# GpSimd and ScalarE put the bias into PSUM in place of a bias matmul, in two large dense layers of a GNN and MoE kernel

## The reference

```
# L0_ffn: 8 experts, hidden 1024, top-2 gates
h = gelu_tanh(einsum('td,edh->teh', x, W1) + b1[None])
y = einsum('teh,eho->teo', h, W2) + b2[None];  out = einsum('te,teo->to', gates, y)
# L2_ffn: 8 experts, hidden 2048, gates from a binary tree of sigmoids
h = gelu(einsum('nd,edh->neh', x, w1) + b1[None])
y = einsum('neh,ehd->ned', h, w2) + b2[None];  out = einsum('ned,ne->nd', y, leaf_probs)
```

## Time and profile before

| what | value |
|---|---|
| three timed runs | 589.77, 591.35, 594.08 us; median 591.35 |
| span of the profiled execution, first to last instruction | 590.4 us |
| median less span | 0.95 us |
| TensorE clock granted, mean | 0.988 |
| PE, DVE, ACT, POOL busy | 557.9, 490.8, 412.2, 15.7 us |
| L0F pipeline, by the chain | about 26.7 to 134.2 us |
| L2F pipeline, by the chain | about 223.7 to 428.1 us |
| L3F pipeline, by the chain | about 468.8 us to the end |

### The profile page before, as it was taken

One profiled execution on the slowest core, in us unless ns is written; L12 is line 12 of the kernel. 1 busy time (PEld: TensorE's weight loads), 2 busy tenths in 40 slices (PEclk: granted clock), 3 DMA queues, 4 the chain that ended last, 5 costly groups with the idle time before them and its releaser, 6 DMA issues.

```text
span 590.4 us, 8259 instructions
## 1 busy us (share of the span) xinstructions
PE 557.9 (94%) x2747; PEld 455.5 (77%) x2747; DVE 490.8 (83%) x475; ACT 412.2 (70%) x411; POOL 15.7 (3%) x40
## 2 busy tenths in 40 slices
PE   5898999997899998999999999999998799999997
PEld 4676888884678887688888888888877588888886
DVE  7799898994659986888988989889987759998996
ACT  4787878772159876878778787787842447878783
POOL 3100000000100000000000000000000100000000
PEclk9999999998899999999999999999999989999999
DMA  8689989995257985689989989998971248999830
GB/s 286 233 313 422 380 328 347 344 329 197 73 172 291 378 304 197 260 325 347 352 330 345 334 345 352 325 354 327 356 284 74 76 163 316 354 353 340 341 121 19
DMA packets 26861, 168.06 MB, mean 285 GB/s; under 512 B 5228, under 2 KB 5357, under 8 KB 6856
## 3 DMA queue, kind: packets, MB, share of 16 engines
q1 hardware_dynamic: 25430, 165.72, 74.5%
q10 hardware_dynamic: 1410, 2.07, 1.1%
HBM read 167.51 MB, written 0.26 MB: 284 GB/s over the span
## 4 chain that ended last, share of the span: by engine, by line
PE 79%; DVE 10%; ACT 5%; issue 3%; POOL 2%; DMA 1%; SPq 0%; POOLq 0%; DVEq 0%; ACTq 0%
PE pre L612 33%; PE y L612 33%; PE tp L624 6%; DVE w_lo L973 3%; ACT w_hi L359 2%; PE pre L619 2%; DVE st L932 1%; POOL rstd L317 1%; PE y L711 1%; DMA ends<-in_edge_weight 1%; ACT L417 1%; DVE XN L951 1%; PE wt L831 1%; PE pre L727 1%; POOL rstd L316 1%
## 5 line engine op out<-in xcount | busy, mean ns | idle before, releaser
L973 DVE TENSOR_TENSOR w_lo<-raw,w_hi 128x2048 fp32r<-128x2048 f32 x151 | 340.0, 2287 | 48.4 <-ACT w_hi L359 48.0
L359 ACT ACTIVATE w_hi<-raw 128x2048 fp32r<-128x2048 f32 x152 | 285.4, 1915 | 0.0
L422 ACT ACTIVATE hT_hi<-tp 128x512 fp32r<-128x512 f32 x66 | 39.5, 599 | 82.0 <-PE tp L624 82.0
L612 PE MATMUL pre<-w_hi,x_hi 128*128 128x512 f32 x292 | 81.4, 401 | 3.7 <-ACT x_hi L373 2.9
L612 PE MATMUL y<-w_hi,hT_hi 128*128 128x512 f32 x280 | 81.7, 413 | 0.0
L612 PE MATMUL pre<-w_lo,x_hi 128*128 128x512 f32 x292 | 80.2, 397 | 1.4 <-DVE w_lo L973 0.9
L612 PE MATMUL pre<-w_hi,x_lo 128*128 128x512 f32 x292 | 78.9, 392 | 0.0
L612 PE MATMUL y<-w_lo,hT_hi 128*128 128x512 f32 x280 | 75.7, 392 | 0.5 <-DVE w_lo L973 0.4
L612 PE MATMUL y<-w_hi,hT_lo 128*128 128x512 f32 x280 | 75.2, 390 | 0.0
L612 PEld LDWEIGHTS pre<-w_hi,x_hi 128*128 128x128 f32 x292 | 54.9, 192 | 17.1 <-issue 3.6
L612 PEld LDWEIGHTS pre<-w_lo,x_hi 128*128 128x128 f32 x292 | 55.6, 192 | 14.8 <-DVE w_lo L973 2.3
(11 more groups left out here) (252 smaller groups left out, 385.8 us busy)
## 6 DMA issues: line engine op xcount, KB each, us to landing
raw<-in_chunks SPq DMA_DIRECT2D x156, 1024.0 KB, 5.5
side<-in_L_gnn_emb ACTq DMA_DIRECT2D x1, 512.0 KB, 3.9
affine<-in_L_ffn_W SPq DMA_DIRECT2D x1, 512.0 KB, 7.3
side<-in_L_ffn_W SPq DMA_DIRECT2D x1, 512.0 KB, 10.1
affine<-in_L_gnn_ln_g ACTq DMA_DIRECT2D x2, 256.0 KB, 4.4
affine<-in_L_gnn_ln_b ACTq DMA_DIRECT2D x2, 256.0 KB, 4.9
X<-in_x ACTq DMA_DIRECT2D x1, 256.0 KB, 2.8
affine<-in_L_gnn_gamma SPq DMA_DIRECT2D x1, 256.0 KB, 5.5
```

What stands on the lines that cost most here:

```text
L359: act.activation(w_hi[:, g % SPLIT_SLOTS], raw[:, g % RAW_SLOTS], ACT.Copy).then_inc(w_hi_ready, 4)
L422: act.activation(hT_hi[:, (s - 1) % 2], tp[:].rearrange("p (c n) -> p c n", n=P), ACT.Copy).then_inc(hT_hi_ready, 1)
L612: last = pe.matmul(dst, xs[:, k], ws[:, k], start=start and i == 0, stop=stop and i == len(passes) - 1 and bias is None)
L973: dve.tensor_tensor(w_lo[:, i], raw[:, g % RAW_SLOTS], w_hi[:, i].bitcast(F32), ALU.subtract).then_inc(w_lo_ready, 4)
```

## The change

For each unit of L0F and L2F, POOL copies one bias row of 512 values onto all 128 partitions (`partition_broadcast`, in `widen`) into one of two buffers, `bias_wide`. ACT copies that buffer into the bank `pre[s % 2]` (`seed_bias`), after the activation of unit s-2 has read the bank. PE waits for that copy (`bias_seeded`) and runs its 12 matmuls with `start=False`, so that they add onto it. The thirteenth matmul, `sel`, and the rounding and halving of the two layers' biases go. The bias row of L2G keeps a matmul; its `bias_hl` is split once, by DVE after the L0F pipeline (`bl_split`). Before L0F, two matmuls of one row by 512 write the two `pre` banks (`pre_opened`). `BRIDGE["l0f"]` goes from 4 to 0. The bias rows come by eight small loads for each layer, one for each expert, in place of two loads of eight rows.

```diff
 # GpSimd
+            def widen(pipe, s):
...
+                if pipe.biased + s > 0:
+                    pool.wait_ge(widened, pipe.biased + s)
+                if pipe.biased + s >= 2:
+                    pool.wait_ge(bias_seeded, pipe.biased + s - 1)
+                pool.partition_broadcast(bias_wide[:, s % 2], rows[32 * (e % 4):32 * (e % 4) + 1, col:col + D],
+                                         channels=P).then_inc(widened, 1)
             for tag in NORMED[1:]:
+                pipe = {"l0f": L0F, "l2f": L2F}.get(tag)
+                if pipe is not None:
+                    if pipe is L0F:
+                        pool.wait_ge(sm("l0_bias_in"), 16 * E8)
+                    else:
+                        pool.wait_ge(sm("l2_bias_in"), 16 * E8)
+                    pool.wait_ge(sm("rstd"), nth("rstd", tag) - 1)
+                    widen(pipe, 0)
+                    widen(pipe, 1)
+                    pool.wait_ge(widened, pipe.biased + 2)
                 inv_std(tag)
+                if pipe is not None:
+                    pool.wait_ge(sm("rstd"), nth("rstd", tag))
+                    for s in range(2, pipe.n):
+                        widen(pipe, s)
+                    pool.wait_ge(widened, pipe.biased + pipe.n)
 # ScalarE, in step s of the pipeline
-                    if pipe.selected is not None and s % 2 == 0 and s < pipe.n and (s >= 4 or s == 0):
-                        select(s // 2, it)
...
                     if s >= 2:
                         round_chunk(g + AHEAD, it)
+                    if pipe.biased is not None and s + 2 < pipe.n:
+                        seed_bias(pipe, s + 2, it)
...
+            def seed_bias(pipe, s, it=None):
+                if s >= 2:
+                    act.wait_ge(h_ready, at(pipe.turned + s - 1, 4, it))
+                act.wait_ge(widened, at(pipe.biased + s + 1, 4, it))
+                act.activation(pre[s % 2][:], bias_wide[:, s % 2], ACT.Copy).then_inc(bias_seeded, 1)
 # ScalarE, before L0F, and after it
-            halve_bias(slice(0, 2 * D), slice(0, 2 * D))
-            halve_bias(slice(BL_COL, BL_COL + D), slice(2 * D, 3 * D))
+            act.activation(bias_hl[0:16, :], l2g_raw, ACT.Copy).then_inc(sm("bias_hi"), 1)
+            act.activation(l2g_raw, l2g_raw, ACT.Copy, scale=half[:, 0:1]).then_inc(sm("bias_hi"), 1)
+            act.wait_ge(sm("pre_opened"), 2)
+            seed_bias(L0F, 0)
+            seed_bias(L0F, 1)
             round_x("l0f", True)
             pipeline(L0F, lambda: exp_logits("l0f", E8))
-            act.wait_ge(sm("l0_bias"), 1)
-            for top in (0, E8):
-                small(scratch[top:top + E8, :], A["L2_ffn_b1"], "bias_in")
+            act.wait_ge(widened, L0F.n)
+            act.wait_ge(sm("bl_split"), 1)
+            for e in range(E8):
+                small((scratch, bias_rows)[e // 4][32 * (e % 4):32 * (e % 4) + 1, :], A["L2_ffn_b1"][e:e + 1, :],
+                      "l2_bias_in")
             small(b2[0:E8, :], A["L1_ffn_b2"], "b2_l1")
             round_x("l1g", False)
 # TensorE
-                if bias is not None:
...
-                    pe.wait_ge(sel_ready, pair)
-                    last = pe.matmul(dst, rows, halves, start=False, stop=True)
...
+                            pe.wait_ge(bias_seeded, at(pipe.biased + s + 1, 4, it))
+                        product(g, pre[s % 2][:], x_hi, x_lo, not biased, True, it, biased, low)
...
+            pe.wait_ge(sm("l0g_swept"), 6)
+            for bank_ap in pre:
+                pe.matmul(bank_ap[:], ident[0:1, :], X[0:1, :], start=True, stop=True).then_inc(
+                    sm("pre_opened"), 1)
 # VectorE, at L0F's start and after its pipeline; four halve_bias in L2G go too
-            dve.wait_ge(sm("bias_hi"), 4)
-            link(halve_bias(slice(0, 2 * D), slice(0, 2 * D)))
-            halve_bias(slice(BL_COL, BL_COL + D), slice(2 * D, 3 * D)).then_inc(sm("l0_bias"), 1)
             split_chunk(1)
...
             pipeline(L0F, route_l0, 1, True, graph_matrices)
+            dve.wait_ge(sm("bias_hi"), 2)
+            hl = bias_hl[0:16, :]
+            dve.scalar_tensor_tensor(out=hl, in0=hl.bitcast(F32), scalar=half[:, 1:2], in1=l2g_raw, op0=ALU.mult,
+                                     op1=ALU.add).then_inc(sm("bl_split"), 1)
             layer_norm("l1g")
```

More of the change, by code:

```diff
@@ L79, in loops @@
         return (self.n - 4) // 4
-L0F = Pipe("l0f", G_L0F, 16, 2, 0, 1, ACT.Gelu_apprx_tanh, selected=0)
-L2F = Pipe("l2f", G_L2F, 32, 4, 16, 1 + 8 + 1, ACT.Gelu, selected=8)
+L0F = Pipe("l0f", G_L0F, 16, 2, 0, 1, ACT.Gelu_apprx_tanh, biased=0)
+L2F = Pipe("l2f", G_L2F, 32, 4, 16, 1 + 8 + 1, ACT.Gelu, biased=16)
 L3F = Pipe("l3f", G_L3F, 18, 2, 16 + 32, 1 + 8 + 1 + 16, ACT.Silu, lead=2)
-BL_COL = 2048
 def arrived(g):
@@ L219, in gnn_ffn_kernel @@
         y_summed = sm("y_summed")
-        sel_ready = sm("sel_ready")
+        widened = sm("widened")
+        bias_seeded = sm("bias_seeded")
         dve_link = sm("dve_link")
@@ L426, in pipeline @@
                     step(s)
-                with act.Fori(0, pipe.loops()) as it:
+                loops = pipe.loops() - (1 if pipe.biased is not None else 0)
+                with act.Fori(0, loops) as it:
                     for s in range(4, 8):
                         step(s, it)
-                for s in range(4 + 4 * pipe.loops(), pipe.n + 2):
+                for s in range(4 + 4 * loops, pipe.n + 2):
                     step(s)
@@ L597, in _, with product @@
         def _(pe):
-            def product(g, dst, xs_hi, xs_lo, start, stop, it=None, bias=None, low=None):
+            def product(g, dst, xs_hi, xs_lo, start, stop, it=None, seeded=False, low=None):
                 hi, lo = w_hi[:, g % SPLIT_SLOTS], w_lo[:, g % SPLIT_SLOTS]
@@ L612, in product @@
                     last = pe.matmul(dst, xs[:, k], ws[:, k], start=start and i == 0,
-                                     stop=stop and i == len(passes) - 1 and bias is None)
-                if bias is not None:
-                    pair, rows, halves = bias
-                    if g in (G_L0F, G_L2F):
-                        pe.wait_ge(*((sm("l0_bias"), 1) if g == G_L0F else (sm("l2_bias"), 4)))
-                    pe.wait_ge(sel_ready, pair)
-                    last = pe.matmul(dst, rows, halves, start=False, stop=True)
+                                     stop=stop and i == len(passes) - 1, skip_group_check=seeded)
                 last.then_inc(chunk_done, 1)
@@ L651, in seed @@
                 pe.wait_ge(sm("gTs"), nth("gTs", tag))
-                return pe.matmul(dst, gT[:], b2[0:E8, :], start=True, stop=tag != "l1f")
+                return pe.matmul(dst, gT, b2[0:E8, :], start=True, stop=tag != "l1f")
             def pipeline(pipe, router, seeded, between=None):
@@ L837, in _ @@
                         pe.wait_ge(sm("l2g_out"), s - 3)
-                    pe.matmul(y[s % 2][:], sel_all[:, 2 * (s - 2) + 1], bias_hl[:, BL_COL:BL_COL + D], start=True,
+                    pe.matmul(y[s % 2][:], sel_all[:, 2 * (s - 2) + 1], bias_hl[:], start=True,
                               stop=False)
@@ L1135, in _ @@
             split_quarter(0, 2)
-            def halve_bias(cols, raw_cols):
-                hl = bias_hl[0:16, cols]
-                return dve.scalar_tensor_tensor(out=hl, in0=hl.bitcast(F32), scalar=half[:, 1:2],
-                                                in1=scratch[0:16, raw_cols], op0=ALU.mult, op1=ALU.add)
             def graph_matrices(s):
```

60 lines of the change are left out of this document (26 added, 34 removed).

## The result

The changed kernel takes 597.01 us (median of 7 runs, 594.87 to 599.59) beside 591.65 us for the kernel before on the same chip (7 runs, 589.77 to 594.08). The ratio is 1.0083, 95% interval 1.0059 to 1.0107: 5.4 us slower, where 1.4 us faster was forecast. The profiled spans are 595.1 and 590.4 us, of one execution each. Times of one kernel go with the mean granted TensorE clock of the execution (its two levels in the records are 1.00 and 0.50): of 35 executions of the kernel before on another chip, those at 0.994 took 588.9 to 590.8 us, those at 0.980 596.1 to 596.9.

A forecast was written before the change was run, and what follows sets the result against it. PE was taken to bound the steady steps, DVE the start-up. Terms -9.0 + 5.3 + 1.45 - 1.0 + 0.73 + 1.0 = -1.5 us gave a forecast of 590.0 us (chance 0.37, own range 586 to 597); 8-in-10 range 581 to 613.

The forecast's parts named there:

- The gain: Steady steps of L0F and L2F: 40 bias matmuls gone at 0.226 us each, 9.0 us saved.
- those ahead of the other layer norms: POOL's code exchanges before the L1G, L2F and L3G norms: hidden in POOL's idling, 0 us; shown instead, 606.3, chance 0.13.
- The opening of the banks: The two `pre_opened` matmuls before L0F run while PE would wait: 0 us.
- the rival: Steady steps: broadcasts between DVE's splits hold the next split, slower by 1% from a 0.57 us hold; chance 0.28.
- the rival's case of half the hold: Steady steps: the broadcast holds DVE's split for half of its 1.1 us, giving 597 us; chance 0.10.
- the step of L0F's start: Net price at L0F's start: later norm +5.3, lower clock +1.45, less bias work -1.0 us.
- the third exchange: POOL's return to broadcasts after L0F's `inv_std`: 5.5 us, broadcast ends 38.6, seed wanted 39.2, just in time, no cost.
- the exchange back: POOL's switch from broadcasts to built-in operations ahead of L0F's `inv_std`: 5.5 us, within the +5.3 for a later norm.
- The lower clock: L0F's start: PE idles some 5 us, then runs at a lower granted clock: +1.45 us.
- the -1.0 for fewer bias splits at the start: L0F's start: DVE loses two `halve_bias`, ACT two `sel` copies but gains four seeds: net -1.0 us.
- the split as forecast: After L0F, DVE's split of the remaining bias stands ahead of L1G's statistics: +0.73 us.
- L2F's start: Four seeds less three `sel` copies on ACT, 1.2 us, taken as +1.0 us.

The follow-up runs named there:

- e1: Changed kernel with the square root of L0F's layer norm on ACT and its reciprocal on DVE, instead of POOL: 591.77 us, ratio to before 0.997.
- e8: Changed kernel with SP holding its loads from the ninth chunk on until the first broadcast behind L0F's norm is done: single time 596.79 us, before 590.91.
- e9: e1 plus L0F's first two broadcasts moved early, e7's order, and the banks opened by two one-pass products amid the counting products: 590.52 us, ratio 0.9972.
- e7: Changed kernel with DVE's graph-layer bias split moved behind the low part of L1G's input, ACT's nine loads behind L1G's activation: 599.58 us, ratio 1.0145.
- e3: Changed kernel with POOL's first two broadcasts moved ahead of its work at 17.6 us: 591.85 us, ratio 0.9977.
- e10: e9 with ACT's nine small loads moved behind its next two roundings and L2F's root on ACT too: 588.84 us, ratio 0.9928.
- e12: e10 with ACT's seed of a unit moved behind the rounding it stood in front of: 587.32 us, ratio 0.9912.

## Why the prediction was wrong

**Right.** The gain: 40 x 0.226 = 9.0 by steps of 5.924 against 6.150, to the third digit. That there are exchanges, three at L0F, and that those ahead of the other layer norms are hidden: in after POOL starts 0.18 us after the statistics' aggregate of L1G ends (145.65 against 145.47), near the 0.1 that I named. The opening of the banks, hidden while PE waited, as I said; it comes out only where the wait is gone (e1's chain).

**Right by size, not by mechanism.** I forecast that DVE does not wait for broadcasts. It does, by 0.47 us a step, as the rival had it (between two splits); it costs nothing because 0.47 is under the 0.57 us from which I had it cost, inside DVE's idle time. That the rival's case of half the hold names 597 us and 597.01 was measured is chance: it would have come from longer steps, and the steps are 5.924.

**Wrong: the step of L0F's start, in three terms.** It was forecast at 5.3 + 1.45 - 1.0 = 5.75 us and measured 10.94, and this 5.2 with the 1.5 of a later norm is the whole miss (-1.5 forecast, +4.7 measured, the other terms within 0.5 together).

The largest is the third exchange, "just in time". It was priced at 5.5, and its end at 38.6 compared with a seed wanted at 39.2: a margin of 0.6 us between two estimates, entered as a cost of zero. It took 10.07 us, because it fell into the moment when SP's loads start again; e8 gives 5.79 without them. The seed waited 3.41 us, and with the queue behind it that cost 2.6 us (after against e8). I wrote what would happen if it were late (ACT's rounding queues behind the seed), which is what happened, and gave that case neither a price nor a chance of its own.

The second is the exchange back, ahead of the root. I took 5.5 for each of the two from small transfers. The one toward broadcasts took 5.81, near that; the one back 7.11, and I had no reason to think the two alike. The root came 7.11 us behind the statistics in place of 0.28, so 6.8 later where 5.3 was forecast. The lower clock, priced at 1.45, was there: the turns of x took 1.11 us in place of 0.66, and from unit 0's first product to the next group 4.16 us passed in place of 3.42, together 1.2. By the figure of the Trainium skill, GPSIMD Engine Reference, section 2.1 (Instruction dispatch), approximately 6 us for the first call to a freshly loaded kernel, the second exchange would have been 1 us short too. The runs have 5.62 to 10.59, and pay it at each change.

The third is the -1.0 for fewer bias splits at the start. Of the 10.94 us the terms above leave 10.94 - 6.8 - 1.2 - 2.6 = 0.3, and without any exchange on the path the start is 1.0 to 2.0 us longer than before (27.77 and 28.80 against 26.80): the sign was wrong. In e9's and e1's timelines ACT has next to no idle time from unit 1 to unit 3, and four seeds of 0.60 stand in it; that it is they is argued, not tested.

**Smaller.** L1G lost 1.73 us up to its first product, 0.74 by the split as forecast and 0.9 by its turns (2.04 us in place of 1.13); from its norm to L2G's it still took no longer than before (29.68 against 30.12). Over the runs that stretch varied from 28.67 to 34.61, and it goes with the granted clock of the table: 28.67 at 0.94, 29.68 to 30.12 at 0.88 to 0.89, 31.01 to 31.93 at 0.78 to 0.84, 34.61 at 0.71, and 1 to 2 us more in e7 and e9, which have ACT's issues on the path. L2F's start was forecast at +1.0 and measured 28 x 0.226 - 5.47 = 0.9, but by luck: six other runs had 2.1, the first broadcast having begun just behind a split.

**What stays open.** What sets the length of an exchange: back to built-in operations it took 6.72 to 7.11 us, but toward broadcasts it took 6.86 to 7.61 in L2G and 5.62 to 6.28 ahead of L0F's norm and behind L2F's, so the direction alone is not it. What brings the granted clock to its low level more often in some runs than in others between L1G and L2G. Most of what L0F won in e1, e3 and e8 and the times do not show stands beside that lower clock (0.84, 0.71 and 0.78 against 0.88); that is an agreement of single executions, not a test.

## What to carry to other kernels

An operation that POOL can begin only after an exchange is priced by its neighbours: 0.8 us of broadcast cost 5.8 to 10 us of standing still ahead of it and 7 behind, so all such work goes together, ahead of a place where POOL idles, and the small operations in between go to another engine. When a forecast says that something is just in time, the late case needs its price and its chance, above all where the wait stands in an in-order queue with other work behind it. And when work is moved off one path, its DMA issues move with it: 2.85 us of issuing on ACT undid e7.

## What the runs showed of the hardware

The exchange: 5.6 to 6.3 us toward broadcasts ahead of L0F's norm and behind L2F's, 6.9 to 7.6 in L2G, 6.7 to 7.1 back, and toward broadcasts behind L0F's norm 9.5 to 10.59, or 5.79 with the loads held. A broadcast of 1 x 512 to 128 x 512 takes 0.80 us alone; begun 0.01 us behind a split with two SBUF inputs it takes 2.96, begun 0.12 us ahead of one it takes 0.80 and the split 2.69 in place of 2.29. The held time follows the order in which the two start, which the Trainium skill's SBUF — State Buffer, section Who interferes with whom, says too, and the sizes are these; begun 0.02 us ahead (e10, e12), the broadcast was still the one held.
